# Products without a reader in the first front's waits and at two places of each joint pass

## The chip, the cores and the metric

One core of a Trainium2 chip runs the whole program. The metric is device microseconds of one execution. Three runs of the kernel before took 849.41 to 850.13 us, median 850.01. The engines are named as the profile names them: PE is TensorE's matrix multiply (PEld its weight load), DVE is VectorE, ACT is ScalarE, POOL is GpSimd and SP is SyncE.

## What is computed

The reference is a small language model of two layers on 16 sequences of 128 tokens, with vectors of 192 numbers, all in float32. It embeds the tokens and mixes word vectors in by a gate. Then, each time as `h = h + part(layernorm(h))`:

```
h += L0_attn : 12 heads; q, k rotated and normed; a linear attention built of three cumulative sums;
               a norm over each head's output; Wo
h += L0_ffn  : a sigmoid score per token; the 19 tokens of lowest score in each sequence get attention (a
               softmax over the keys), the others a mixture with a pooled vector; then a norm and a
               192 -> 768 -> 192 feed-forward
h += L1_attn : low-rank q, k, v; a softmax attention of 12 heads
h += L1_ffn  : 8 experts, the best 2 of each token, 192 -> 768 -> 192 each, weighted sum
```

## The kernel before

The 16 sequences are worked on in four groups of four (`G = 4`, `NG = 4`). Each engine has its own program, an order written out by hand; the engines meet only through semaphores that count up (`w(turn, name, n)` waits until the semaphore `name` has reached `n` in this turn, `inc` raises it). Each engine's program is cut into three kinds of pieces. `front(0)` takes the first group through the first layer up to its selection of tokens and its mixture. `joint(ta, tb)` runs three times: it takes group `ta` through the same work, and between its steps group `tb = ta - 1` through the feed-forward, the second layer's attention and the routing to experts. `back(3)` takes the last group through that second half, and then the tiles of the experts run.

The order on PE is set by `front` (line 2302), `joint` (2376) and `back` (2504). The steps that matter here, in their order:

- In the front: `cumulate` (cumulative sums of the scores), `qk_turn` (transposes of q and k), `kq`, `av` and `ob_T` (the attention, sequence by sequence), `on_T` (transpose of the normed heads, after DVE's head norm, L1342), `wo` (output projection), `n3_T` (transpose of the third norm), `scores` (after the router's exponential on ACT and its reciprocal on DVE, L1376: one sum `ssum`, then the scores broadcast over the partitions, `bc`), `keys`, `values`, `select` (products with the one-hot matrix of the chosen tokens, 20 columns each), `queries` (after ACT's copy of `select`, `selT`, L760), `select_T`, `words_T` and `word_vectors` (for the next group's embedding), `route_logits` (the chosen tokens' attention logits; DVE takes their maxima at L1426), `mix` (the mixture), `probs_T`, `context`, `selected` and `attn`.
- In a joint pass, at the fifth norm (the norm before the second layer's attention): `ffn_down(tb, 0..3)`, `qk_turn(ta, 0, 0..2)`, `kq(ta, 0)`, `x5_T(tb, 0)` and `x5_T(tb, 1)` (transposes of the normed rows, each block waiting for DVE's L1114), and then `qk_turn(ta, 1, j)` in turn with `qk1(tb, n)` (the projections to q and k). `qk_turn(ta, 1, 0)` waits for DVE's masks (L1318), which read `kq(ta, 0)`; `qk1` waits for ACT's copies of `x5_T` (L810).
- In a joint pass, at the selection: `values(ta, 1)`, `gate(tb)` (the experts' logits, 8 columns each), `select(ta)`, `queries(ta)`, `counts(tb)`, `select_T`, `route_logits`, then as in the front. On DVE `pooled` (L1413, L1415) waits for `selT`, and behind it stand the routing of `tb`, `head_queries` (L1420) and the maxima.

A product with no reader is one of two helpers. It multiplies the first 32 columns of the identity by a resident weight, and writes 32 partitions of a bank in which at that time nothing stands that is still to be read:

```python
def stream(n):                      # 512 columns, always bank PC[:, 0]
    mm(PC[0:32, 0, :], ident[:, 0:32], w_l0[:, 0, 0:512])
def hold(bank, n):                  # 256 columns, the bank named
    mm(bank[0:32, 0:256], ident[:, 0:32], w_1q[:, 0, 0:8, :].rearrange(...))
```

(each in a loop of `n`; neither waits for a semaphore nor raises one). In the kernel before, `front` has streams at seven places, and `joint` and `back` have holds at many. PSUM is two tensors of four banks, `QA` and `QC`; PA, PB are the halves of `QA` and PC, PD those of `QC`. In the profile every matmul has line 1930 and every transpose 1933, so steps are told apart by their operands. A float32 product shows as two records. The profile names the weight of `stream` arena_e, that of `hold` w_1q.

Of the kernel before, what the change touches and what calls it, by code (L numbers as in the profile page):

```python
# [76 lines left out]
def build(nc, a, out):  # L77
    with ExitStack() as ctx:
# [182 lines left out]
        QA, QC = (ctx.enter_context(nc.psum_tensor(n, [128, 4, 512], F32)) for n in ("qa", "qc"))  # L261
# [1666 lines left out]
        def _(pe):  # L1928
# [103 lines left out]
            def ob_T(ta, b, wide=False):  # L2032
                w(ta, "pv_e", b + 1)
                for j in range(3):
                    i = tr(lin(b, wide)[:, 3, j * 128:(j + 1) * 128], ob[:, b % 2, j, :], 128)
                inc(i, "o_T")

            def on_T(ta, hf):
                for b in (2 * hf, 2 * hf + 1):
                    w(ta, "hln", 18 + b + 1)  # L2040
                    for c in range(C):
                        i = tr(part_of(PA, CW, b, c), onrm[:, b, c * CW:(c + 1) * CW], 128)
                    inc(i, "onT")
# [250 lines left out]
            def stream(n):  # L2294
                for _ in range(n):
                    mm(PC[0:32, 0, :], ident[:, 0:32], w_l0[:, 0, 0:512])
# [5 lines left out]
            def front(ta):  # L2302
                stream(4)
                x1_T(ta, 0)
                x1_T(ta, 1)
                proj(ta, 0)
                proj(ta, 1)
                proj(ta, 2)
                proj(ta, 3)
                stream(4)  # L2310
                prior_sums(ta, 0)
                prior_sums(ta, 1)
                prior_sums(ta, 2)
                prior_sums(ta, 3)
                stream(1)
                scores_T(ta)
                stream(3)
                scores_back(ta)
                cumulate(ta)
                stream(4)  # L2320
                qk_turn(ta, 0, 0, True)
                qk_turn(ta, 0, 1, True)
                qk_turn(ta, 0, 2, True)
                qk_turn(ta, 1, 0, True)
                qk_turn(ta, 1, 1, True)
                qk_turn(ta, 1, 2, True)
                kq(ta, 0, True)
                kq(ta, 1, True)
                av(ta, 0, True)
                qk_turn(ta, 2, 0, True)  # L2330
                qk_turn(ta, 2, 1, True)
                qk_turn(ta, 2, 2, True)
                ob_T(ta, 0, True)
                av(ta, 1, True)
                qk_turn(ta, 3, 0, True)
                qk_turn(ta, 3, 1, True)
                qk_turn(ta, 3, 2, True)
                ob_T(ta, 1, True)
                kq(ta, 2, True)
                kq(ta, 3, True)  # L2340
                av(ta, 2, True)
                ob_T(ta, 2, True)
                av(ta, 3, True)
                ob_T(ta, 3, True)
                on_T(ta, 0)
                on_T(ta, 1)
                wo(ta, 0)
                wo(ta, 1)
                pe.wait_ge(ld_ffn, 176)
                stream(6)  # L2350
                n3_T(ta, 0)
                n3_T(ta, 1)
                stream(2)
                scores(ta)
                keys(ta)
                values(ta, 0)
                values(ta, 1)
                select(ta)
                queries(ta)
                select_T(ta)  # L2360
                words_T(ta + 1)
                route_logits(ta, 0)
                route_logits(ta, 1)
                word_vectors(ta + 1)
                mix(ta, 0)
                mix(ta, 1)
                probs_T(ta, 0)
                probs_T(ta, 1)
                context(ta, 0)
                context(ta, 1)  # L2370
                selected(ta, 0)
                selected(ta, 1)
                attn(ta, 0)
                attn(ta, 1)

            def joint(ta, tb):
                x1_T(ta, 0)
                x1_T(ta, 1)
                proj(ta, 0)
                proj(ta, 1)  # L2380
                proj(ta, 2)
                proj(ta, 3)
                n4_T(tb, 0)
                prior_sums(ta, 0)
                prior_sums(ta, 1)
                n4_T(tb, 1)
                prior_sums(ta, 2)
                prior_sums(ta, 3)
                ffn_up(tb, 0)
                ffn_up(tb, 1)  # L2390
                ffn_up(tb, 2)
                scores_T(ta)
                ffn_up(tb, 3)
                ffn_up(tb, 4)
                ffn_up(tb, 5)
                scores_back(ta)
                cumulate(ta)
                ffn_down(tb, 0)
                ffn_down(tb, 1)
                ffn_down(tb, 2)  # L2400
                ffn_down(tb, 3)
                qk_turn(ta, 0, 0)
                qk_turn(ta, 0, 1)
                qk_turn(ta, 0, 2)
                kq(ta, 0)
                x5_T(tb, 0)
                x5_T(tb, 1)
                qk_turn(ta, 1, 0)
                qk1(tb, 0)
                qk_turn(ta, 1, 1)  # L2410
                qk1(tb, 1)
                qk_turn(ta, 1, 2)
                qk1(tb, 2)
                qk1(tb, 3)
                av(ta, 0)
                qk1(tb, 4)
                qk1(tb, 5)
                ob_T(ta, 0)
                kq(ta, 1)
                v1_rows(tb, 0)  # L2420
                v1_rows(tb, 1)
                qk_turn(ta, 2, 0)
                logits(tb, 0)
                qk_turn(ta, 2, 1)
                qk_turn(ta, 2, 2)
                av(ta, 1)
                max_T(tb, 0)
                ob_T(ta, 1)
                logits_T(tb, 0)
                kq(ta, 2)  # L2430
                av1(tb, 0)
                qk_turn(ta, 3, 0)
                o_T(tb, 0)
                qk_turn(ta, 3, 1)
                qk_turn(ta, 3, 2)
                logits(tb, 1)
                av(ta, 2)
                ob_T(ta, 2)
                max_T(tb, 1)
                logits_T(tb, 1)  # L2440
                kq(ta, 3)
                av1(tb, 1)
                o_T(tb, 1)
                hold(QC[:, 3, :], 1)
                logits(tb, 2)
                av(ta, 3)
                hold(QA[:, 2, :], 2)
                max_T(tb, 2)
                ob_T(ta, 3)
                logits_T(tb, 2)  # L2450
                hold(QA[:, 2, :], 3)
                av1(tb, 2)
                hold(QC[:, 3, :], 1)
                o_T(tb, 2)
                on_T(ta, 0)
                on_T(ta, 1)
                logits(tb, 3)
                wo(ta, 0)
                wo(ta, 1)
                max_T(tb, 3)  # L2460
                hold(QC[:, 3, :], 5)
                logits_T(tb, 3)
                hold(QA[:, 2, :], 1)
                n3_T(ta, 0)
                n3_T(ta, 1)
                av1(tb, 3)
                hold(QC[:, 3, :], 1)
                o_T(tb, 3)
                scores(ta)
                keys(ta)  # L2470
                values(ta, 0)
                x6_T(tb, 0)
                x6_T(tb, 1)
                values(ta, 1)
                gate(tb)
                select(ta)
                hold(QC[:, 3, :], 2)
                queries(ta)
                hold(QC[:, 3, :], 1)
                counts(tb)  # L2480
                select_T(ta)
                route_logits(ta, 0)
                if ta + 1 < NG:
                    words_T(ta + 1)
                route_logits(ta, 1)
                gates_T(tb)
                if ta + 1 < NG:
                    word_vectors(ta + 1)
                hold(QC[:, 3, :], 5)
                mix(ta, 0)  # L2490
                mix(ta, 1)
                bias_rows(tb, 0)
                probs_T(ta, 0)
                probs_T(ta, 1)
                context(ta, 0)
                bias_rows(tb, 1)
                context(ta, 1)
                hold(QC[:, 3, :], 2)
                selected(ta, 0)
                selected(ta, 1)  # L2500
                attn(ta, 0)
                attn(ta, 1)
# [141 lines left out]
            for g in range(NG - 1):  # L2644
                joint(g + 1, g)
# [106 lines left out]
```

## Time and profile before

| | |
|---|---|
| median of three runs | 850.01 us |
| the profiled execution's own time | 846.64 us |
| its span, first to last instruction | 844.8 us |
| PE busy | 734.1 us, 87% |
| DVE busy | 505.8 us, 60% |
| ACT busy | 300.7 us, 36% |
| POOL busy | 232.8 us, 28% |
| mean granted clock of PE | 0.968 |

Busy times overlap between engines. A busy PE counts time with a matmul in the array, at whichever clock was granted; the clock is granted at 1.00 (2.4 GHz) or at half of it (1.2 GHz), and a figure between is a mean over a stretch. The page's chain that ended last has 55% of the span on PE and 23% on DVE.

### The profile page before, as it was taken

The page shows a single profiled execution, that of the slowest core. Times are in us where ns is not written, and L with a number is a line of the kernel's source. Part 1 is how long each engine was busy: PE and PEld are TensorE (multiplying, and loading weights), DVE is VectorE, ACT ScalarE, POOL GpSimd, SP SyncE. Part 2 cuts the span into 40 slices and gives each one's busy share as a digit, 9 for nine tenths or more (in the row PEclk, how much of TensorE's full clock was granted, in tenths as well). Part 3 has the DMA queues.
Part 4 walks back from the last instruction along what each step waited for, and adds up shares of the span by engine and source line. Part 5 has one row for each costly group of instructions (what it writes and reads, how often), then busy time and mean ns, then how long its engine had stood idle before and what let it go on. Part 6 is the DMA issues. An engine that isn't in the chain of part 4 may idle for free.

```text
span 844.8 us, 15945 instructions
## 1 busy us (share of the span) xinstructions
PE 734.1 (87%) x5710; PEld 542.6 (64%) x5711; DVE 505.8 (60%) x1707; ACT 300.7 (36%) x698; POOL 232.8 (28%) x281
## 2 busy tenths in 40 slices
PE   1798777989889998988998898899989999999992
PEld 0545455466657646655764665675856989999992
DVE  6558668773769787367977546884345543333330
ACT  0024132433443262434416244333333433333330
POOL 5242110452001346100322200132001454443442
PEclk9899999999999999999999999989999999999997
DMA  7960000000000100000010000016601233222220
GB/s 252 415 282 1 1 1 1 19 8 1 2 2 3 56 19 8 1 3 1 20 39 1 1 1 2 2 38 255 213 2 30 44 76 49 38 43 35 42 32 9
DMA packets 29621, 43.22 MB, mean 51 GB/s; under 512 B 5146, under 2 KB 24451, under 8 KB 29556
## 3 DMA queue, kind: packets, MB, share of 16 engines
q1 hardware_dynamic: 19264, 30.98, 10.4%
q0 software_dynamic: 8432, 8.53, 5.8%
q10 hardware_dynamic: 1860, 2.84, 0.9%
q8 instruction: 41, 0.67, 0.3%
q14 instruction: 24, 0.20, 0.1%
HBM read 20.92 MB, written 22.09 MB: 51 GB/s over the span
## 4 chain that ended last, share of the span: by engine, by line
PE 55%; DVE 23%; issue 6%; POOL 4%; DMA 4%; ACT 4%; SPq 1%; DVEq 0%; POOLq 0%; ACTq 0%
PE qa L1930 25%; PE qc L1930 24%; PE qc L1933 4%; PE qa L1933 3%; DMA out<-qk_T 3%; DVE mx L1506 2%; DVE st L1070 2%; DMA mu_row<-in_mu 1%; ACT big L824 1%; DVE arena_e L1318 1%; POOL arena_w L444 1%; DVE qk_T L1512 1%; ACT wT L791 1%; POOL rs_a L479 1%; DVE ctxT L1461 1%
## 5 line engine op out<-in xcount | busy, mean ns | idle before, releaser
L1930 PE MATMUL qc<-arena_w,big 128*128 x468 | 83.0, 327 | 2.1 <-DVE qk_T L1909 1.4
L1930 PEld LDWEIGHTS qc<-arena_w,big 128*128 128x128 f32 x468 | 75.1, 190 | 3.3 <-issue 3.2
L1930 PE MATMUL qa<-arena_e,nT 128*128 128x192 f32 (+2 forms) x256 | 69.3, 426 | 2.3 <-DVE ga L1388 2.0
L1930 PE MATMUL qa<-arena_b 128*128 128x128 f32 (+2 forms) x688 | 69.9, 281 | 1.0 <-ACT arena_b L781 0.8
L621 POOL DMA_INDIRECT out<-qk_T x39 | 63.7, 1633 | 19.6 <-POOL spare L620 9.9
L1036 ACT ACTIVATE big<-qa,arena_b 128x128 f32<-128x128 f32 x156 | 43.0, 375 | 72.2 <-PE qc L1930 67.3
L1930 PEld LDWEIGHTS qa<-arena_b 128*128 128x128 f32 (+2 forms) x688 | 64.0, 187 | 6.4 <-ACT arena_b L781 1.4
L1930 PEld LDWEIGHTS qa<-arena_e,nT 128*128 128x128 f32 x256 | 45.9, 195 | 24.8 <-issue 14.6
L1909 DVE TENSOR_SCALAR qk_T<-qc,qk_T 128x192 f32<-128x192 f32 x39 | 16.3, 417 | 65.3 <-PE qc L1930 60.4
L479 POOL TENSOR_TENSOR rs_a<-rs_a,minus_half 128x8 f32<-128x8 f32 x4 | 6.6, 1642 | 170.8 <-DVE rs_a L1355 170.8
L1933 PE MATMUL qa<-cst,arena_b 128*128 128x128 f32 (+2 forms) x232 | 33.7, 286 | 9.5 <-DVE arena_e L1318 4.0
L1930 PE MATMUL qc<-w_1q,cst 128*32 128x256 f32 x152 | 41.1, 400 | 0.0
L1506 DVE TENSOR_REDUCE mx<-qc 128x6 f32<-128x768 f32 x28 | 25.5, 954 | 23.9 <-PE qc L1930 23.9
L1933 PEld LDWEIGHTS qa<-cst,arena_b 128*128 128x128 f32 (+2 forms) x232 | 25.9, 143 | 20.3 <-issue 10.9
L716 ACT ACTIVATE arena_e<-qa 128x512 f32<-128x512 f32 x42 | 23.3, 596 | 43.6 <-PE qa L1933 43.5
L824 ACT ACTIVATE big<-qc 128x768 f32<-128x768 f32 x28 | 21.2, 808 | 43.7 <-PE qc L1930 43.7
L1930 PE MATMUL qc<-qk_T 32*128 32x128 f32 (+1 forms) x680 | 29.3, 290 | 8.0 <-DVE qk_T L1512 5.3
L524 POOL TENSOR_TENSOR arena_b<-arena_w,ck 128x576 f32<-128x576 f32 x16 | 18.5, 1164 | 61.5 <-DVE cf L1288 48.3
L541 POOL DMA_INDIRECT slots<-xk,pos_i x32 | 32.3, 1010 | 10.3 <-issue 10.0
L1930 PE MATMUL qc<-arena_e,big 128*128 128x192 f32 x192 | 32.3, 328 | 2.8 <-ACT big L797 2.8
L1930 PEld LDWEIGHTS qc<-qk_T 32*128 32x128 f32 (+1 forms) x680 | 23.7, 187 | 16.9 <-DVE qk_T L1512 10.1
L1930 PE MATMUL qc<-wT,arena_e 128*128 128x512 f32 (+3 forms) x88 | 31.3, 595 | 3.4 <-ACT wT L791 3.2
(393 smaller groups left out, 1555.7 us busy)
## 6 DMA issues: line engine op xcount, KB each, us to landing
slots<-xk SPq DMA_DIRECT2D x1, 13192.0 KB, 41.3
arena_e<-in_w SPq DMA_DIRECT2D x8, 579.0 KB, 7.6
arena_w<-in_w SPq DMA_DIRECT2D x8, 576.0 KB, 8.5
qk_T<-slots SPq DMA_DIRECT2D x39, 97.0 KB, 2.0
out<-hb SPq DMA_DIRECT2D x16, 96.0 KB, 1.7
arena_e<-in_w_l SPq DMA_DIRECT2D x1, 816.0 KB, 8.1
arena_e<-in_W ACTq DMA_DIRECT2D x1, 768.0 KB
out<-qk_T POOLq DMA_INDIRECT x39, 3.6
```

The costliest lines, as they stand in the source:

```text
L479: pool.tensor_tensor(rs_a[:, 1, :, :], rs_a[:, 0, :, :], minus_half.rearrange("p (k b) -> p k b", k=2), ALU.pow).then_inc(s["rstd_a"], 1)
L524: pool.tensor_tensor(qk48[:, b % 2, 1, :, 0:48].rearrange("p h (k d) -> p h k d", k=3), bc(rq[:, b, H:24, :], 2, 3), bc(ck[:, b, :, :], 3, ...
L541: pool.indirect_dma_start(out=slots, out_offset=bass.IndirectOffsetOnAxis(ap=pos_i[:, k, b:b + 1], axis=0), in_=xk[:, k, b, :], in_offset= ...
L621: pool.indirect_dma_start(out=rows_out, out_offset=bass.IndirectOffsetOnAxis(ap=xs[:, u, D + 1:D + 2].bitcast(I32), axis=0), in_=ym[:, u, ...
L716: A(qkTf[:, b % 2, j * 512:(j + 1) * 512], lin(b, wide)[:, j, :], ACT.Copy).then_inc(*done("qk_evac"))
L824: A(eT[:, b % 2, 6 * hf:6 * hf + 6, :].rearrange("p (i j) t -> p i (j t)", i=2), sec(b, wide)[:, 2 * hf:2 * hf + 2, 0:384], ACT.Exp, scale ...
L1036: i = A(hTm[:, u % 2, j, :], PS[u % 2][:, j % 2, j // 2 * 128:j // 2 * 128 + 128], ACT.Gelu, bias=w1s[u % 3][:, F + FJ // 2 * 128 + j:F + ...
L1070: nc.vector.bn_stats(st[:, b, :], src[:, b, :]).then_inc(s[name], 1)
L1506: nc.vector.reduce_max(mx1[:, :, HD].rearrange("p (j i) -> p i j", i=4)[:, 2 * hf:2 * hf + 2, :], sec(b, wide)[:, 2 * hf:2 * hf + 2, 0:384 ...
L1909: TS(ym[:, u, :], PD[:, 1, 0:D], xs[:, u, D:D + 1], None, ALU.mult).then_inc(m_y, 1)
L1930: return nc.tensor.matmul(o, l, r, start=start, stop=stop)
L1933: return nc.tensor.transpose(o, i, ident[0:k, 0:k])
```

## The change

At the places shown, more products without a reader are issued on PE. Nothing else changes: no wait, no other engine, no order among the other steps.

```diff
 def front(ta):
...
                 scores_back(ta)
                 cumulate(ta)
-                stream(4)
+                stream(6)
                 qk_turn(ta, 0, 0, True)
...
                 ob_T(ta, 3, True)
+                hold(QC[:, 0, :], 5)
                 on_T(ta, 0)
                 on_T(ta, 1)
                 wo(ta, 0)
...
                 n3_T(ta, 0)
                 n3_T(ta, 1)
-                stream(2)
+                stream(5)
                 scores(ta)
                 keys(ta)
                 values(ta, 0)
                 values(ta, 1)
+                hold(QC[:, 0, :], 1)
                 select(ta)
+                hold(QC[:, 0, :], 2)
                 queries(ta)
                 select_T(ta)
+                hold(QC[:, 0, :], 1)
                 words_T(ta + 1)
                 route_logits(ta, 0)
                 route_logits(ta, 1)
                 word_vectors(ta + 1)
+                hold(QC[:, 0, :], 4)
                 mix(ta, 0)
+                hold(QC[:, 0, :], 2)
                 mix(ta, 1)
                 probs_T(ta, 0)
                 probs_T(ta, 1)
                 context(ta, 0)
                 context(ta, 1)
+                hold(QC[:, 0, :], 2)
                 selected(ta, 0)
...
 def joint(ta, tb):
...
                 qk_turn(ta, 0, 2)
+                hold(QC[:, 3, :], 2)
                 kq(ta, 0)
+                hold(QC[:, 3, :], 1)
                 x5_T(tb, 0)
+                hold(QC[:, 3, :], 1)
                 x5_T(tb, 1)
+                hold(QC[:, 0, :], 1)
                 qk_turn(ta, 1, 0)
                 qk1(tb, 0)
...
                 gate(tb)
+                hold(QC[:, 3, :], 2)
                 select(ta)
                 hold(QC[:, 3, :], 2)
                 queries(ta)
```

## Rows read from the trace of the kernel before

**Rows 1.** The profile's page, its first line: span and instructions.

```profile
span 844.8 us, 15945 instructions
```

**Rows 2.** Stages: length, busy us (instructions) by engine, PEclk, DMA share, GB/s.

```profile
90.00:130.00 40.00, 31.23 (x156) 20.67 (x145) 24.92 (x105) 12.59 (x25) 6.44 (x9) 0.87 0.00 0
184.00:195.00 11.00, 8.96 (x48) 5.27 (x47) 7.82 (x21) 3.37 (x8) 7.57 (x10) 0.69 0.00 0
264.00:270.00 6.00, 6.00 (x38) 3.99 (x38) 5.38 (x38) 2.17 (x7) 0.00 (x0) 0.72 0.01 3
...
476.00:482.00 6.00, 4.80 (x17) 2.78 (x18) 3.58 (x6) 1.84 (x4) 0.49 (x1) 0.72 0.00 0
552.00:560.00 8.00, 8.00 (x39) 6.25 (x38) 6.75 (x45) 1.72 (x5) 0.98 (x2) 0.57 0.00 1
```

**Rows 3.** PE in order of time, front: start, us, instruction [wait <-releaser].

```profile
72.62 1.53 PE L1933 MATMUL qa<-cst,arena_b 128*128 128x128 f32 x12 [2.10 <-DVE arena_b L1311]
...
94.62 1.59 PE L1933 MATMUL qa<-cst,arena_b 128*96 128x128 f32 x8 [3.00 <-DVE arena_b L1342]
96.00 4.15 PE L1930 MATMUL qa<-arena_e,nT 128*128 128x192 f32 x16
...
112.38 0.59 PE L1930 MATMUL qa<-zz,cst 128*128 128x4 f32 x2 [3.15 <-DVE zz L1376]
112.83 2.05 PE L1930 MATMUL qa<-arena_w,cst 128*128 128x128 f32 x8
114.67 4.12 PE L1930 MATMUL qa<-nT,arena_e 128*96 128x512 f32 x8
...
121.23 1.46 PE L1930 MATMUL qa<-pw,xn 128*96 128x20 f32 x16
123.59 0.87 PE L1930 MATMUL qa<-selT,arena_e 128*96 128x76 f32 x8 [0.90 <-ACT selT L760]
...
126.52 3.31 PE L1930 MATMUL qa<-arena_b,arena_w 96*114 96x128 f32 x16
...
141.64 1.48 PE L1930 MATMUL qa<-arena_e,ctxT 128*19 128x192 f32 x8 [1.05 <-DVE ctxT L1461]
```

**Rows 4.** PE in order of time, fifth norm of the three passes.

```profile
185.11 1.61 PE L1930 MATMUL qa<-arena_e 48*128 48x128 f32 x24 [0.79 <-ACT arena_e L716]
...
189.99 1.08 PE L1933 MATMUL qa<-cst,arena_b 128*128 128x128 f32 x4 [0.29 <-DVE arena_e L1318]
190.87 3.55 PE L1930 MATMUL qc<-xT,w_1q 128*128 128x512 f32 x4
...
202.98 1.88 PE L1930 MATMUL qc<-xT,w_1k 128*128 128x512 f32 x4
...
334.58 3.38 PE L1930 MATMUL qc<-xT,w_1q 128*128 128x512 f32 x4
...
479.08 2.81 PE L1930 MATMUL qc<-xT,w_1q 128*128 128x512 f32 x4
```

**Rows 5.** PE, ACT and DVE in order of time, selection, first and third pass.

```profile
264.00 1.51 PE L1930 MATMUL qa<-pw,xn 128*96 128x20 f32 x16
...
265.55 0.72 ACT L760 ACTIVATE selT<-qa,cols 96x80 f32<-96x80 f32 x2
...
266.66 0.21 DVE L1413 TENSOR_SCALAR ptmp<-ga,cols 96x4 f32<-96x4 f32 x1
...
558.98 0.42 DVE L1426 TENSOR_REDUCE nx<-qa 114x2 f32<-114x256 f32 x1 [0.63 <-PE qa L1930]
```

**Rows 6.** PE in order of time, first joint pass, at full clock.

```profile
241.81 2.87 PE L1930 MATMUL qa<-arena_e,nT 128*128 128x192 f32 x16
...
244.93 2.35 PE L1930 MATMUL qc<-w_1q,cst 128*32 128x256 f32 x10
...
253.50 1.16 PE L1930 MATMUL qa<-arena_w,cst 128*128 128x128 f32 x8
...
270.26 1.04 PE L1930 MATMUL qa<-arena_b,arena_w 96*114 96x128 f32 x8
```

## The prediction, made before the kernel was run

> **What bounds the kernel now.** I first read the profiled execution's own time beside its span: 846.64 us for a span of 844.8 [rows 1], so 1.8 us lie around the span, and the timed runs' median, 850.01, is 3.37 longer than this execution. I make the sum against 846.64 and carry the difference over to the median.
>
> Second, the table of stages, for TensorE's granted clock. Between 90 and 560 us it is below 1.00 in seven stretches, and a stretch's share below 1.00, doubled, is the time at 1.2 instead of 2.4 GHz: 10.4 us in the front (0.13 of 40 us, twice), 6.8 and 3.4 in the first joint pass, and 3.4 and 6.9 in the third [rows 2]; the second pass has two more that read like the row at 264. That is 37.7 us in all. The reader is to see that they lie at three kinds of place: the front from its output projection to its mixture, the fifth norm of each pass (184, 333, 476), and the selection of each pass (264, 408, 552).
>
> Third, PE's order of time, for what PE did before each of them. In the front PE waited 3.00 us for VectorE's head norm before `on_T`, 3.15 for the router's reciprocal before `scores`, and short waits stand around the selection [rows 3]. At the fifth norm there are four waits one behind the other, the first 0.79 and the last 0.29 [rows 4]. At the selection PE waits for nothing: `gate` and `select` issue matmuls of 8 and 20 columns, which keep the queue busy with little in each [rows 5]. Elsewhere in these passes the chain of waits goes through PE and VectorE in turn, so a microsecond that PE gains before a VectorE step is mostly a microsecond of the end.
>
> **What the change does, and each price.** It removes and moves nothing; it adds 5 products of 512 columns (`stream`) and 17 of 256 (`hold`) in the front, and 7 holds in each of three passes, 38 holds in all. No DMA, no wait and no work on another engine is added; what can be late is only what stands behind a product on PE. A hold is two records; five of them take 2.35 us at full clock, 0.47 each with the modelled end [rows 6]. A stream has twice the columns: 0.94, an estimate from that row. At half clock each would be double.
>
> Front, cover. `stream(6)` adds 2 x 0.94 = 1.88 into a wait of 2.10; the five holds before `on_T` 2.35 into 3.00; the three streams 2.82 into 3.15; the two holds before `queries` 0.94 into 0.90, 0.04 over; the last, before `selected`, 0.94 into 1.05 [rows 3]. The other three (before `words_T` and the two halves of `mix`) lie in waits of the same table that are longer than their products. The engine that ends each wait is VectorE or ScalarE, so these cost nothing, and if the cover were gone each would cost its own duration. Only the hold before `select` has no wait in front of it [rows 3]: 0.47 us on the path. Front, products without cover: +0.5.
>
> Front, clock. With the first wait filled I take the clock to stay at 2.4 GHz over `on_T` and `wo`. `wo` took 4.15 and the same sixteen records at full clock in a joint pass 2.87 [rows 3, 6]: 1.3 us, and VectorE's residual add waits for its last product. After the second, `scores`' broadcasts took 2.05 against 1.16 at full clock, 0.9, and of the keys' 4.12 about 0.5 was lost: 1.4. After the third, the route's logits took 3.31 against twice 1.04: 1.2; VectorE's four maxima behind them can follow only at their own pace, so I count 1.1. What is late next in each case is a VectorE chain that starts from that product, and it moves up with it. Front: 1.3 + 1.4 + 1.1 - 0.5 = 3.3 us less.
>
> Fifth norm, cover. Two holds, 0.94, stand in 0.79 before `kq(0)`, so `kq` comes up to 0.15 late; `kq` was done at 186.7, and VectorE's mask, which reads it, comes behind the four normalisations and released PE's transposes only at 189.99 [rows 4]. One hold before each half of `x5_T`, and one before `qk_turn(1, 0)`, stand in waits of about their size; the last is 0.29 with the transposes ahead at half clock and grows when these are faster. ScalarE's copy of the second half is still what releases the projections. I take 0; the ends are 0 and the overrun of all four, about 0.5 a pass.
>
> Fifth norm, clock. The first projection took 3.55, 3.38 in the second pass and 2.81 in the third, and 1.88 at full clock: 1.7, 1.5 and 0.9 [rows 4]. The transposes before it, 1.08 for four records where half of that would do, give back some 0.3 more a pass. From 190.87 to the row of 202.98 and the seven between them PE has no wait, so this reaches the attention behind, whose steps start from PE. Together 5.0 us less.
>
> Selection. Two holds stand before `select` with no wait there, so `select` comes 0.94 late. ScalarE's copy of it ended at 265.55 + 0.72 = 266.27, and VectorE took it up at 266.66 [rows 5]: 0.39 of slack, the rest, 0.55, moves VectorE, which from there to the mixture hardly waits. What the clock gives back at this place (slower holds and `queries`) lies on PE beside VectorE's dense chain, so in the first two passes I count none of it: +0.55 each. In the third VectorE waited 0.63 for the route's logits, which ran at half clock [rows 5], and PE goes on to the mixture without a wait; there the kept clock gives between 0.1 (that wait less the late `select`) and 2.5 (half of 6.9 less two holds), and I take 1.0, nearer the VectorE row. Selection: 0.55 + 0.55 - 1.0 = +0.1.
>
> Sum: -3.3 - 5.0 + 0.1 = -8.2 us. 846.6 becomes 838.4, and the median 850.0 becomes **841.8**.
>
> One rule speaks for more. The Trainium skill (TensorE: Matmul & The Clock Gate, Terms) puts the penalty of time at a reduced clock at that time multiplied by the missing share of the clock, whatever PE was doing. For 37.7 us at one half it gives 18.9, and by it the sum would be about -17. The rows above show less at each place, since PE waited in a part of each stretch.
>
> **Rivals.**
> A. The clock is kept only in part, or VectorE takes the place of PE. The holds before `select` are few against the small matmuls around them, so at the selection the clock may still fall; then the two holds after `select` run at half clock behind a late `select`, and each pass loses about 1.5 us instead of 0.55. And behind the fifth norm some of the 5 us may be waited for elsewhere. Front -3.3, half of 5.0, selection +3 x 0.55: -4.2, **846**. For it: VectorE is busy 5.38 of 6 us at the selection [rows 2]. Against it: behind the fifth norm PE alone sets the pace for 14 us [rows 4].
> B. Slower: the products don't hold the clock, since they fill 32 output columns. Then the clock falls as before, and the holds at half clock overrun: at the fifth norm the last takes 0.94 in a wait of 0.29, and with the one before it about 1.1 a pass; at the selection 1.5 a pass; in the front 0.5. Sum 3 x 2.6 + 0.5 = +8.3, **858**. It decides if the stretches of [rows 2] still read below 1.00. Against it: the five holds of [rows 6] run at full clock, and so does what follows them, the broadcasts at 1.16.
> C. All of PE's lost time is on the path: half of 37.7 us is 18.9, less the 0.5 and 1.7 of uncovered products: -16.7, **833**. That is also what the rule of the skill gives. Against it: `wo` lost 1.3 in a stretch where the rule has 1.7, and VectorE's waits at the selection are nearly none.
> D. The change doesn't do what it says, because the clock falls a little later in place of where it fell: gains and losses cancel, **850**.
>
> **How the numbers follow.** The forecast has 0.62 with its own range 838 to 845; A 0.22, B 0.06, C 0.04, D 0.06. A range from 836.5 to 847.5 leaves out B, C, D and a small part of the first two. It takes in the uncovered products (up to 0.5 a pass at the fifth norm), the third pass's 0.1 to 2.5, and a median that loses up to the 3.37 us to the clock that the profiled execution did not. About 0.2%, 1.7 us, can be told from no change: faster 0.87 (forecast, C and nearly all of A), same 0.06, slower 0.07.
>
> **What would show it.** The stage table should read a clock of 1.00 from 90 to 560 us but for some of the selections. PE's waits of 3.00 and 3.15 should be under 1 us, `wo` near 2.9, the broadcasts near 1.2, the route's logits near 2.1, and all three first projections of the fifth norm 1.9. VectorE should wait some 0.5 us for the copy of `select`. The passes, from one input transpose to the next, should be about 1 us shorter and the front about 3. The prediction is wrong if the clock still falls at the fifth norms, or if it stays up and the front and the passes are no shorter.

## The result, and the profile after

The changed kernel took 843.16 us, median of five runs (840.25 to 844.55), against 849.41 (848.0 to 850.13) for the kernel before. The ratio is 0.9926, interval 0.9903 to 0.9950: 0.7% or 6.2 us faster, clear of no change. The forecast was 841.8 and 8.2 us less. The profiled execution is the slowest of the five: 844.55 us, span 842.7, only 2.1 us less than the profiled one of before. The medians are 6.2 apart and the profiles 2.1, because the profiled execution of before was 2.8 under its median and this one is 1.4 over. Its mean granted clock is 0.983 (before 0.968).

The table of stages of the changed kernel (length, busy us and instructions by engine, PEclk, DMA share, GB/s), for the stretches of [rows 2], which begin earlier now, and for everything from the front to the third selection:

```profile
90.00:130.00 40.00, 37.04 (x178) 20.88 (x179) 28.32 (x119) 15.11 (x39) 6.45 (x9) 1.00 0.00 1
180.00:191.00 11.00, 10.82 (x65) 5.91 (x64) 7.69 (x21) 4.38 (x8) 7.70 (x10) 1.00 0.01 1
254.00:266.00 12.00, 11.29 (x88) 9.13 (x87) 10.55 (x72) 3.90 (x10) 1.27 (x3) 1.00 0.01 2
465.00:477.00 12.00, 10.66 (x65) 5.85 (x64) 6.72 (x17) 4.18 (x8) 3.29 (x3) 1.00 0.00 1
539.00:555.00 16.00, 16.00 (x91) 12.86 (x89) 11.91 (x76) 3.90 (x10) 2.06 (x5) 0.68 0.01 2
60.00:539.00 479.00, 431.81 (x3428) 282.83 (x3429) 344.20 (x1177) 188.81 (x364) 105.59 (x129) 1.00 0.03 8
```

The reader is to see that eight of the nine falls are gone, and that the ninth, at the third selection, is longer: 0.32 of 16 us, doubled, is 10.2 us at 1.2 GHz, where it was 6.9 (0.43 of 8 us, doubled [rows 2]).

PE in order of time, front of the changed kernel:

```profile
72.00 1.53 PE L1933 MATMUL qa<-cst,arena_b 128*128 128x128 f32 x12 [0.39 <-DVE arena_b L1311]
...
90.94 2.35 PE L1930 MATMUL qc<-w_1q,cst 128*32 128x256 f32 x10
94.00 1.23 PE L1933 MATMUL qa<-cst,arena_b 128*96 128x128 f32 x8 [0.72 <-DVE arena_b L1342]
95.38 2.87 PE L1930 MATMUL qa<-arena_e,nT 128*128 128x192 f32 x16
...
110.48 0.39 PE L1930 MATMUL qa<-zz,cst 128*128 128x4 f32 x2 [0.59 <-DVE zz L1376]
110.81 1.16 PE L1930 MATMUL qa<-arena_w,cst 128*128 128x128 f32 x8
111.80 3.60 PE L1930 MATMUL qa<-nT,arena_e 128*96 128x512 f32 x8
...
117.93 0.62 PE L1930 MATMUL qc<-w_1q,cst 128*32 128x256 f32 x2
118.48 1.53 PE L1930 MATMUL qa<-pw,xn 128*96 128x20 f32 x16
...
120.92 0.90 PE L1930 MATMUL qa<-selT,arena_e 128*96 128x76 f32 x8
...
123.57 1.91 PE L1930 MATMUL qa<-arena_b,arena_w 96*114 96x128 f32 x16
...
137.51 1.48 PE L1930 MATMUL qa<-arena_e,ctxT 128*19 128x192 f32 x8
```

Beside [rows 3]: the waits of 2.10, 3.00 and 3.15 are down to 0.39, 0.72 and 0.59, with products in them, and the waiting steps start when VectorE lets them. `wo`, the broadcasts, the keys and the route's logits run at 2.4 GHz: 4.15 to 2.87, 2.05 to 1.16, 4.12 to 3.60, 3.31 to 1.91.

PE at the fifth norm of the first and third pass of the changed kernel:

```profile
181.09 1.61 PE L1930 MATMUL qa<-arena_e 48*128 48x128 f32 x24
...
185.25 0.62 PE L1930 MATMUL qc<-w_1q,cst 128*32 128x256 f32 x2
185.86 0.63 PE L1933 MATMUL qa<-cst,arena_b 128*128 128x128 f32 x4
186.32 1.88 PE L1930 MATMUL qc<-xT,w_1q 128*128 128x512 f32 x4
...
470.94 0.64 PE L1933 MATMUL qc<-cst,xb 128*96 128x128 f32 x4
471.51 0.62 PE L1930 MATMUL qc<-w_1q,cst 128*32 128x256 f32 x2
472.06 0.66 PE L1933 MATMUL qa<-cst,arena_b 128*128 128x128 f32 x4
472.56 1.88 PE L1930 MATMUL qc<-xT,w_1q 128*128 128x512 f32 x4
```

Beside [rows 4]: the transposes 1.08 to 0.63, the first projection 3.55 and 2.81 to 1.88. In the third pass the last holds have no wait to stand in. The kernel before had one of 0.53 us in front of these transposes:

```profile
478.20 1.09 PE L1933 MATMUL qa<-cst,arena_b 128*128 128x128 f32 x4 [0.53 <-DVE arena_e L1318]
```

The selection of the changed kernel, first and third pass, in order of time (PE, ACT, DVE):

```profile
256.10 1.85 PE L1930 MATMUL qc<-w_gate,xT 128*128 128x8 f32 x16
257.88 1.05 PE L1930 MATMUL qc<-w_1q,cst 128*32 128x256 f32 x4
258.86 1.53 PE L1930 MATMUL qa<-pw,xn 128*96 128x20 f32 x16
260.43 0.72 ACT L760 ACTIVATE selT<-qa,cols 96x80 f32<-96x80 f32 x2 [1.01 <-PE qa L1930]
261.18 0.23 DVE L1413 TENSOR_SCALAR ptmp<-ga,cols 96x4 f32<-96x4 f32 x1 [0.63 <-ACT selT L760]
...
543.95 2.29 PE L1930 MATMUL qa<-pw,xn 128*96 128x20 f32 x16
546.18 1.92 PE L1930 MATMUL qc<-w_1q,cst 128*32 128x256 f32 x4
547.04 0.23 DVE L1413 TENSOR_SCALAR ptmp<-ga,cols 96x4 f32<-96x4 f32 x1 [1.39 <-ACT selT L760]
549.98 1.17 DVE L1420 TENSOR_TENSOR arena_w<-qTs,cst 96x456 f32<-96x456 f32 x2 [0.73 <-ACT qTs L766]
551.61 0.19 DVE L1584 COPY tot<-qc 128x32 f32<-128x32 f32 x1 [0.46 <-PE qc L1930]
```

Where [rows 5] had no wait at L1413, VectorE now waits 0.63 us in the first pass for ScalarE's copy of the late `select`. In the third the clock fell during `select`, and VectorE waits 1.39, 0.73 and 0.46 for things that PE gave at half clock.

The two traces put together by VectorE's rows. Each length, in us, runs from the start of a group's or pass's first row of one line to that of another. L1253 is a scaling of the scores in the front, L1461 the reduction that ends the context, L1495 the residual add behind the feed-forward, L1506 the maxima of the second layer's logits, and L1393 the ranking of the tokens.

| stretch | before | after | difference |
|---|---|---|---|
| span's start to the front's L1253 | 61.45 | 60.83 | -0.6 |
| front, L1253 to L1461 | 78.73 | 75.20 | -3.5 |
| fifth norm, L1495 to L1506, three passes | 31.10, 30.71, 31.06 | 29.02, 29.03, 30.23 | -2.1, -1.7, -0.8 |
| selection, L1393 to L1461, three passes | 24.55, 24.58, 22.37 | 25.11, 25.25, 25.05 | +0.6, +0.7, +2.7 |
| third L1461 to PE's last product | 261.7 | 263.3 | +1.7 |
| PE's last product to the span's end | 14.0 | 15.0 | +1.0 |

Everything between these is the same to 0.02 us (40.10 against 40.12 from the first pass's L1461 to the next L1495). The differences add up to the 2.1 us, but for rounding. From one L1461 to the next, the first two passes are 1.5 and 1.0 us shorter, and the third is 1.9 longer.

### The profile page after: what moved, and what is told of

Read it like the earlier page. It is cut to its first block, busy times and chain, and to the rows that moved or that the text cites. A ratio compares the mean times of both kernels' runs of the same rounds, so it can differ in the third digit from the quotient of the medians.

```text
span 842.7 us, 16117 instructions
## 1 busy us (share of the span) xinstructions
PE 745.2 (88%) x5796; PEld 542.3 (64%) x5797; DVE 506.3 (60%) x1707; ACT 301.0 (36%) x698; POOL 233.9 (28%) x281
## 3 DMA queue, kind: packets, MB, share of 16 engines
q1 hardware_dynamic: 19264, 30.98, 10.4%
## 4 chain that ended last, share of the span: by engine, by line
PE 53%; DVE 23%; issue 7%; DMA 6%; POOL 4%; ACT 4%; SPq 1%; POOLq 0%; DVEq 0%; ACTq 0%
PE qa L1930 24%; PE qc L1930 23%; DMA out<-qk_T 5%; PE qc L1933 4%; PE qa L1933 3%; DVE mx L1506 2%; DVE st L1070 2%; DMA mu_row<-in_mu 1%; ACT big L824 1%; POOL arena_w L444 1%; DVE qk_T L1512 1%; ACT wT L791 1%; POOL rs_a L479 1%; DVE ctxT L1461 1%; POOL slots L541 1%
## 5 line engine op out<-in xcount | busy, mean ns | idle before, releaser
L1930 PE MATMUL qc<-w_1q,cst 128*32 128x256 f32 x228 | 60.6, 390 | 0.0
L1506 DVE TENSOR_REDUCE mx<-qc 128x6 f32<-128x768 f32 x28 | 25.5, 954 | 23.9 <-PE qc L1930 23.9
L824 ACT ACTIVATE big<-qc 128x768 f32<-128x768 f32 x28 | 21.2, 808 | 43.7 <-PE qc L1930 43.7
L1933 PEld LDWEIGHTS qa<-cst,arena_b 128*128 128x128 f32 (+2 forms) x232 | 24.8, 139 | 14.7 <-issue 9.0
L1930 PEld LDWEIGHTS qc<-w_1q,cst 128*32 128x32 f32 x228 | 21.4, 110 | 19.7 <-issue 6.1
```

The costliest lines, as they stand in the source:

```text
L824: A(eT[:, b % 2, 6 * hf:6 * hf + 6, :].rearrange("p (i j) t -> p i (j t)", i=2), sec(b, wide)[:, 2 * hf:2 * hf + 2, 0:384], ACT.Exp, scale ...
L1506: nc.vector.reduce_max(mx1[:, :, HD].rearrange("p (j i) -> p i j", i=4)[:, 2 * hf:2 * hf + 2, :], sec(b, wide)[:, 2 * hf:2 * hf + 2, 0:384 ...
L1930: return nc.tensor.matmul(o, l, r, start=start, stop=stop)
L1933: return nc.tensor.transpose(o, i, ident[0:k, 0:k])
```

## Experiments

In each run the stretches of the table are read again, in one profiled execution of each kernel. Here are all of them, with each pass's selection and, in brackets, how long the clock was at half there (us). The ratios are of medians, of 5 to 12 executions of each changed kernel:

| kernel | ratio to before (interval) | front | fifth norm | selection |
|---|---|---|---|---|
| before | | 78.73 | 31.10, 30.71, 31.06 | 24.55 (3.4), 24.58 (3.4), 22.37 (6.8) |
| changed | 0.9926 (0.9903 to 0.9950) | 75.20 | 29.02, 29.03, 30.23 | 25.11 (0), 25.25 (0), 25.05 (10.2) |
| after_again | 0.9930 (0.9915 to 0.9946) | 75.17 | 29.02, 29.04, 30.23 | 25.11 (0), 28.52 (10.2), 22.55 (3.4) |
| e1_front | 0.9948 (0.9927 to 0.9969) | 75.18 | 29.03, 30.43, 30.67 | 24.84 (3.4), 24.85 (3.4), 21.19 (3.4) |
| e2_fifth | 0.9996 (0.9969 to 1.0023) | 80.77 | 29.02, 29.02, 30.22 | 27.52 (10.2), 24.51 (0), 23.98 (10.2) |
| e3_select | 1.0077 (1.0047 to 1.0107) | 81.50 | 29.02, 29.03, 30.85 | 25.10 (0), 28.53 (10.2), 25.06 (10.2) |
| e4_no_select | 0.9892 (0.9855 to 0.9930) | 75.18 | 29.02, 29.03, 30.23 | 24.36 (0), 24.68 (3.4), 21.00 (0) |
| e4_again | 0.9910 (0.9876 to 0.9944) | 75.20 | 29.04, 30.16, 30.24 | 24.39 (0), 25.37 (3.4), 23.98 (10.2) |
| e5_small | 1.0000 (0.9978 to 1.0022) | 81.44 | 29.02, 30.16, 32.46 | 24.37 (0), 24.50 (0), 22.69 (6.8) |
| e6_third | 0.9916 (0.9898 to 0.9935) | 75.18 | 29.03, 29.02, 31.77 | 24.85 (3.4), 25.89 (6.8), 22.60 (0) |
| e7_turns | 0.9905 (0.9883 to 0.9927) | 75.19 | 29.03, 29.02, 31.76 | 24.68 (0), 24.81 (0), 24.61 (10.2) |
| e8_after | 0.9916 (0.9886 to 0.9946) | 75.20 | 29.03, 29.02, 30.24 | 25.83 (3.4), 25.87 (3.4), 22.46 (3.4) |

**Is it the clock?** The changed kernel with products of 8 columns at the same places:

```diff
+def small(bank, n):
+    for _ in range(n):
+        mm(bank[0:32, 0:8], ident[:, 0:32], w_1q[:, 0, 0, 0:8])
...
-                hold(QC[:, 0, :], 5)
+                small(QC[:, 0, :], 5)
                 on_T(ta, 0)
...
```

> The changed kernel with as many products at the same places, but of 8 columns each, so that they take next to no time in the array. Theory 1, what helps is PE's array kept at work, by which the clock stays up: the clock falls at the front and the fifth norms again, the front takes 78 us or more, the fifth norms 30.7 to 31.1, and the time is that of the kernel before, ratio 0.997 to 1.003. Theory 2, what helps is that PE's queue isn't left waiting, at whatever clock: ratio 0.994 or less, as with the whole products.

Measured: 848.27, ratio 1.000 (0.9978 to 1.0022). Stages and PE's order of time of this kernel:

```profile
90.00:131.00 41.00, 33.18 (x181) 22.35 (x180) 24.75 (x103) 12.25 (x23) 6.45 (x9) 0.83 0.00 1
```

```profile
91.99 0.48 PE L1930 MATMUL qc<-w_1q,cst 128*32 128x8 f32 x10
95.05 1.94 PE L1933 MATMUL qa<-cst,arena_b 128*96 128x128 f32 x8 [2.58 <-DVE arena_b L1342]
96.82 4.50 PE L1930 MATMUL qa<-arena_e,nT 128*128 128x192 f32 x16
```

As many instructions in the same places, but the wait stays at 2.58, the clock falls, `wo` takes 4.50, and the whole gain is gone. What helps is the array at work, and the clock that stays up with it, not that PE's queue has instructions in it. The first pass's fifth norm did without a fall here (29.02): a place may be spared in one execution.

**One part alone.** The front's products, the fifth norm's, and those before `select`, each alone in the kernel before.

> Only the front's products (five streams, seventeen holds); the joint passes as before. Theory 1, the gains of the places add up: the front is 3.5 us shorter as in the profile of the changed kernel, the six falls of the clock in the passes stay, 846.0 against 849.4 (ratio 0.996). Theory 2, the front's part is given back behind it, since the passes wait for something else: 849, ratio 1.000, with the first pass longer by what the front gained.

Measured: 844.33 against 848.62, 4.3 us less, a little more than the 3.5 of the first theory; the front 75.18, as it forecast. Six falls stay behind the front, but not at the same six places: the first pass's fifth norm had none (29.03, with no product there), and one came at 144 us, in the projections that open the first joint pass.

> Only the five holds at each fifth norm; front and selection as before. Theory 1: 2.1, 1.7 and 0.8 us less in the three passes, 4.6 in all, 844.8 against 849.4 (ratio 0.9946), with the front's three falls and the selection's three in the profile. Theory 2, VectorE takes the place of PE behind it: under 2 us, ratio above 0.9975.

Measured: 848.0 against 848.62, not told from no change, though each fifth norm took exactly what it takes in the changed kernel. In the profiled execution (848.44) the time went elsewhere, in falls at places that the edit doesn't touch: the front took 80.8 and two selections were at half clock for 10.2 us, as this kernel's stages show:

```profile
262.00:275.00 13.00, 13.00 (x71) 10.44 (x72) 9.55 (x60) 4.40 (x15) 2.03 (x3) 0.61 0.03 10
...
549.00:562.00 13.00, 13.00 (x68) 9.81 (x68) 9.89 (x60) 4.24 (x17) 2.23 (x3) 0.61 0.02 8
```

The first theory was right at the place and missed the total. So the fifth norm's part is shown at its place, and not in a total by itself.

> Only the two holds before select in each pass. Theory 1, they cost 0.6 us a pass through the late copy of select, whatever the clock does in the first two passes, and give back up to 2 us in the third only if the clock stays up there: between 848.5 and 851.5, ratio 0.999 to 1.0025. Theory 2, they are worth their cost because the clock is kept: 847 or less, ratio below 0.9975.

Measured: 854.91 against 848.62, 6.3 us slower; both theories missed. With the two holds a pass with no fall takes 25.1 against 24.4 without them, the 0.6 to 0.7 us of the late `select`. But in two of three passes the clock fell all the same, in the middle of `select`, and stayed down for 10.2 us. Second pass of this kernel:

```profile
400.00:420.00 20.00, 19.34 (x110) 15.40 (x109) 14.67 (x91) 6.61 (x19) 4.21 (x7) 0.74 0.02 6
```

```profile
406.71 1.05 PE L1930 MATMUL qc<-w_1q,cst 128*32 128x256 f32 x4
407.69 2.07 PE L1930 MATMUL qa<-pw,xn 128*96 128x20 f32 x16
409.70 1.92 PE L1930 MATMUL qc<-w_1q,cst 128*32 128x256 f32 x4
411.54 1.56 PE L1930 MATMUL qa<-selT,arena_e 128*96 128x76 f32 x8
```

In this profile the front, which the edit doesn't touch, took 2.8 us more than in the profile of before, so the 6.3 need not be all the edit's; why all eight executions took as long (853.0 to 855.9) isn't shown.

**The change without that part.** As the changed kernel, but no hold before `select` in `joint`:

```diff
                 gate(tb)
-                hold(QC[:, 3, :], 2)
                 select(ta)
```

> The change without the two holds before select. Theory 1: VectorE takes up the copy of select without a wait again, 1.2 us less in the first two passes than the changed kernel, though the clock falls there; in the third pass a fall of the size of before, 6.9 us at half clock or less. 841 to 842 (ratio 0.990 to 0.992) against 843.2 for the changed kernel. Theory 2, without them the falls cost what they give: 845 or more, ratio above 0.9945.

> The change without the two holds before select, once more. Theory 1: faster than the changed kernel, 837 to 841, ratio 0.987 to 0.991; the stretch from ranks to the context 24.4 us where the clock stays, 24.5 to 24.9 with a fall of 3.4 us, 27.5 with one of 10.2; third pass 21.0, 21.2 and 24. Theory 2, the first run of it was a lucky one: 842 to 844, ratio 0.992 to 0.995.

Measured: 838.94 against 848.62, better than the first theory had it, and the second time, on another chip, 842.44 against 848.07, as its second theory had it in microseconds; its ratio, 0.991, still lies in the range of the first. So the first result was perhaps in part a lucky draw. In the first profile the clock fell once from 60 to 580 us, for 3.4 us; VectorE took up the copy of `select` with no wait:

```profile
60.00:400.00 340.00, 306.09 (x2431) 200.40 (x2432) 248.98 (x859) 132.65 (x255) 82.01 (x102) 1.00 0.03 8
400.00:408.00 8.00, 8.00 (x53) 5.85 (x53) 7.09 (x47) 3.22 (x9) 0.19 (x1) 0.79 0.01 3
408.00:580.00 172.00, 157.19 (x1184) 104.29 (x1183) 116.31 (x413) 68.72 (x146) 38.96 (x49) 1.00 0.11 41
```

In the second it fell three times, among them for 10.2 us at the third selection. Both ratios are below the changed kernel's two (0.9926 and 0.9930), but the intervals overlap.

> The changed kernel once more, beside the others of this call. Its time 842 to 845, ratio 0.990 to 0.995. Theory 1: the stretch from ranks to the context in the passes takes 25.1 to 25.3 us where the clock stays, and 27 or more where it falls there; the fifth norms 29.0; the front 75.2, whatever the total.

Measured: 842.33 against 848.88, the same as the first time, with the long fall in the second pass instead of the third.

**Other ways to fill the selection.** Four holds in the third pass alone; `gate` and `values(ta, 1)` in turn with one hold; and the two holds behind `select`.

```diff
                 gate(tb)
+                if ta == NG - 1:
+                    hold(QC[:, 3, :], 4)
                 select(ta)
```

> Products in the front and at the fifth norm; before select none in the first two passes and four in the third. Theory 1, the two holds were too few for the clock and are late for VectorE: with four the clock stays in the third pass, and its stretch from ranks to the context takes 22 to 22.6 us instead of 25.1, the first two passes 24.4 to 24.9 each: 839 to 841, ratio 0.989 to 0.991. Theory 2, no number of holds there is worth its time, since the stretch without any takes 21.0 to 22.4 whether or not the clock falls for 3.4 or 6.8 us: slower than the kernel without them by 1 us or more.

Measured: 842.19 against 848.88. The clock stayed in the third pass and the stretch took 22.60, as forecast; but that is more than the 21.0 to 21.2 of e1_front and e4_no_select, which had no hold there and no fall or a short one. So the second theory holds for the stretch: four holds cost more there than a fall of 3.4 or 6.8 us (21.2 and 22.4). The total of the first theory (839 to 841) didn't come: the clock fell at 144 us, in the projections that open the first joint pass, in the first two selections, and at the third fifth norm (31.77).

```diff
-                values(ta, 1)
-                gate(tb)
+                values(ta, 1, (2,))
+                gate(tb, (0, 1))
+                values(ta, 1, (3,))
+                gate(tb, (2, 3))
+                hold(QC[:, 3, :], 1)
                 select(ta)
```

> No two holds before select; the four blocks of gate and the two of values(ta, 1) in turn on PE (values, two of gate, values, two of gate), and one hold before select. Theory 1, the clock falls at the selection because gate and select follow one another with little in the array, so work between them keeps it up at the price of one hold, which VectorE's 0.39 us of slack covers: 24.4 us in each of the first two passes and 21.0 in the third with few falls, 837 to 839, ratio 0.987 to 0.989. Theory 2, the falls stay: as without the holds, 838 to 841, ratio 0.988 to 0.992.

Measured: 841.25 against 848.88. No fall in the first two selections, 24.7 and 24.8; the long one in the third, 24.61, and one at the third fifth norm, 31.76 in spite of its holds. The first theory's total (837 to 839) didn't come. Not told from the kernel without holds.

```diff
                 select(ta)
-                hold(QC[:, 3, :], 2)
+                hold(QC[:, 3, :], 4)
                 queries(ta)
```

> As without the two holds before select, but with two more behind it, four before queries. Theory 1, the price of the holds before select is the late copy of select, so behind it they cost VectorE little: with no fall 24.4 to 24.7 us, and the queries come 0.9 us later, still before VectorE takes them; 838 to 841, ratio 0.988 to 0.991. Theory 2, what costs is any product on PE in this stretch, because at half clock each takes twice its time: 842 to 845, ratio 0.992 to 0.996.

Measured: 842.41 against 848.07. VectorE has no wait at L1413, but in each pass the clock fell behind `select`, the four holds ran in part at half clock, and VectorE waited for the queries:

```profile
261.60 0.21 DVE L1413 TENSOR_SCALAR ptmp<-ga,cols 96x4 f32<-96x4 f32 x1
...
265.15 1.17 DVE L1420 TENSOR_TENSOR arena_w<-qTs,cst 96x456 f32<-96x456 f32 x2 [1.35 <-ACT qTs L766]
```

25.8 us in the first two passes: the second theory held for the stretch, and the place was moved, not the price removed. What four holds behind `select` cost with no fall isn't shown.

## Why the prediction came out as it did

The time lay in the range, and the forecast's mechanism is shown where PE waits: with the array at work in the waits the clock stays, and with 8-column products in their place the gain is zero. That 843.2 came so near 841.8 is in part luck. The three places gave 4.2 us less in the profile of the changed kernel (3.5 + 4.6 - 3.9) and 3.5 in that of after_again, where 8.2 were counted; rival A's -4.2 is the same number from other parts. That the medians lie 6.2 apart goes with the execution of before from which the sum was made: it was among the quick ones, with a span of 844.8 us where 53 later executions of that kernel have a median of 846.8.

- **Front, 3.3 us less:** this held, 3.5 in the profile, and the front took 75.2 us in all eight profiles with its products. `wo` gave 1.3 as forecast. The cover held: each filled wait is still a wait, or starts on time, and `queries` came late by next to nothing. The hold before `select` is the one that stood in no wait.
- **Fifth norm, 5.0 us less:** 4.6, as 2.1, 1.7 and 0.8. The third pass gave less than the 1.2 counted (0.9 and 0.3), because there the cover, taken as 0, failed by about the half microsecond that was its other end. VectorE's last normalised block comes 9.4 us after the start of L1495 both before and after, but the holds behind it put the transposes ahead of the projection at 10.9 us instead of 10.4. Nor does a fifth norm always need the products: without whole ones there (before, e1_front, e3_select, e5_small) it took 29.0 us in four of twelve passes, with them 29.0, or 30.2 in the third, in 21 of 24.
- **Selection, 0.1 us more:** this step failed. The 0.55 for a pass whose clock stays was right: 0.6 and 0.7, with the wait of 0.63 at L1413 to show for it. Wrong was the third pass, where the kept clock was to give between 0.1 and 2.5 and 1.0 was taken: the clock wasn't kept, and the pass lost 2.7 us. Nor does e6_third, where four holds kept it, show a gain (22.60 against 22.37); without holds and without a fall the pass took 21.00. Rival A had said that the holds are few against the small matmuls around them; it priced a pass with a fall at 1.5 us more, and one with a fall of 10.2 us took 2.7 to 4 more than in the kernel before. With two holds before `select`, in the three profiles of kernels that had them in all passes, the clock fell in five of nine selections, four of them for 10.2 us. Without, in before, e1_front, e2_fifth and both of e4, it fell in eleven of fifteen, three of them for 10.2 us. So it is not shown that the holds bring on the long falls; their price without a fall, 0.6 to 0.7 us, is.
- **Not in the sum:** the experts' part, 1.7 us longer in the profile, and the end behind PE, 1.0. In after_again these were 0.4 and 0.7, in e4_no_select 0 and 0.2, and over all twelve profiles the first ran from 261.3 to 263.4 us and the second from 13.8 to 15.5, so they go with the execution; nothing ties them to the edit.
- **Rival C**, half of all the time at half clock: no. In the profile some 27 us at half clock went (37.7 less 10.2), 24 of them in the front and the fifth norms, which got 8.1 us back with them. In the first two selections a fall of 3.4 us costs next to nothing: 24.4 to 24.5 us without one and without holds before `select`, 24.55 to 24.85 in six of seven such stretches with one, because VectorE's chain is the longer there. The same shows without any edit: in 53 timed executions of the kernel before, a straight line of the span (841.0 to 853.2 us) over the time at half clock, worked out from the mean granted clock, rises by 0.27 us per us. The Trainium skill (TensorE: Matmul & The Clock Gate, Terms) puts the penalty at the time at a reduced clock times the missing share of the clock, here one half. The traces and runs of this case show less: about a third at the front and the fifth norms, about a quarter over the executions.
- **Rival B**, that products of 32 columns don't hold the clock, is out by the stage table. **Rival D**, that gains and losses cancel, is out for the whole change by its ratio, and for the front by e1_front; its mechanism, falls that come elsewhere, is seen in e2_fifth.

What stays open: whether the kernel without the holds before `select` is faster than the changed one (0.989 and 0.991 against 0.993 twice), what the fifth norm's holds are worth in a total by themselves, and why some falls at the selection last 10.2 us and others 3.4. In the twelve traces the eight falls of 10.2 us all begin 0.5 to 1.1 us after the first product of `select`, which runs 1.5 us at full clock, and the fifteen shorter ones 1.2 us after it or later; the cause wasn't tried.

## What to carry to other kernels

A product without a reader is worth its place where PE waits for another engine and the work behind the wait is on the path; the wait must be longer than the product, and both are read from one row. Where PE has no wait but only small matmuls, a filler is late work for whoever reads next, and should be tried alone: here two of them cost 0.6 to 0.7 us in a pass even where the clock stayed up. And where the clock falls in one place and not in another from one execution to the next, compare stretches, not totals of single profiles.

## What was not expected

- Under one and the same code the clock falls at different places in different executions. The front as it was before took 78.73, 80.77 and 81.50 us (before, e2_fifth, e3_select), and 81.44 with products of 8 columns. Places that no edit touched had falls where the kernel before had none: the projections that open the first joint pass (`proj`, 384 columns), at 144 us, in e1_front, e6_third and e8_after, 1.7 us longer each, and the second pass's feed-forward at 313 us in e4_again. The stage and `proj` in e1_front, and `proj` in the changed kernel, where it had no fall:

```profile
143.00:149.00 6.00, 5.41 (x14) 3.10 (x15) 0.83 (x4) 1.42 (x3) 0.00 (x0) 0.72 0.00 0
144.07 12.82 PE L1930 MATMUL qa<-arena_e,nT 128*128 128x384 f32 x32
...
144.58 11.13 PE L1930 MATMUL qa<-arena_e,nT 128*128 128x384 f32 x32
```

- A fall of 10.2 us that begins in the short matmuls of `select` costs far more than three times one of 3.4: a selection of the first two passes took 27.5 to 28.5 us with the one, 24.6 to 24.9 with the other (25.4 once), and 24.4 to 24.5 with neither, all but the 28.5 without holds before `select`.
